# Building a product of two weight matrices: the second operand turned by VectorE instead of TensorE

## What is computed

```python
# part 1 (64 experts)
h   = silu(inp @ wg[e]) * (inp @ wu[e]);  out_e = h @ wd[e]
x   = x + scatter(out_e * weight)

# part 2: x is [32, 128, 1024]
H      = einsum('btd,od->bto', x, W)          # + rank-16 adapter picked per batch
result = einsum('bsd,od->bso', H, base_w) + base_b
logits = H @ router_w.T + router_b            # top 2 of 8
x      = x + result + 2 * gated (H @ lora_A) @ lora_B
```

## Time and profile before

| | us |
|---|---|
| median of 3 runs | 2355.13 |
| lowest, highest | 2351.75, 2357.51 |
| the profiled execution, device time | 2365.02 |
| its span in the trace | 2363.3 |
| TensorE busy | 2326.7 (98%) |
| VectorE busy | 1780.2 (75%) |
| ScalarE busy | 1418.5 (60%) |

### The profile page before, as it was taken

How to read it: one execution, slowest core, us unless ns; L and a number is a source line. 1 busy time by engine, 2 the same in 40 slices (tenths; PEclk the granted TensorE clock), 3 DMA queues, 4 the chain that set the end, 5 groups by cost and what they waited for, 6 DMA issues and landing times.

```text
span 2363.3 us, 35497 instructions
## 1 busy us (share of the span) xinstructions
PE 2326.7 (98%) x12594; PEld 2044.4 (87%) x12594; DVE 1780.2 (75%) x3091; ACT 1418.5 (60%) x2349; POOL 1343.8 (57%) x999
## 2 busy tenths in 40 slices
PE   6989999999999999999999999999999999999999
PEld 4768788888888888888888888888889999999999
DVE  4887788888888888888888888888863267666665
ACT  4766677777767777777777776777763122222221
POOL 4117888777777777877778777787730011111110
PEclk9999999999999999999999999999999999999999
DMA  8999899989999989989899899899886444544452
GB/s 300 380 311 335 257 281 288 287 272 292 279 289 290 281 276 283 286 280 279 276 291 282 275 285 279 281 282 287 274 255 140 103 110 131 144 131 132 132 140 83
DMA packets 250307, 582.35 MB, mean 246 GB/s; under 512 B 82697, under 2 KB 106634, under 8 KB 250130
## 3 DMA queue, kind: packets, MB, share of 16 engines
q1 hardware_dynamic: 183154, 401.18, 51.6%
q0 software_dynamic: 55584, 160.02, 26.2%
q10 hardware_dynamic: 11392, 18.88, 2.1%
HBM read 456.25 MB, written 123.45 MB: 245 GB/s over the span
## 4 chain that ended last, share of the span: by engine, by line
PE 94%; DVE 2%; issue 2%; ACT 1%; DMA 1%; ACTq 0%; POOL 0%; SPq 0%; DVEq 0%; POOLq 0%
PE ps L861 26%; PE ps L874 22%; PE ps L860 13%; PE ps L986 9%; PE ps L979 7%; PE ps L931 5%; PE ps L857 4%; PE ps L730 2%; PE ps L969 2%; PE ps L858 2%; PE ps L740 1%; PE ps L943 1%; PE ps L753 1%; PE ps L752 0%; ACT HR L1215 0%
## 5 line engine op out<-in xcount | busy, mean ns | idle before, releaser
L861 PE MATMUL ps<-XX,HR 128*128 128x512 f32 x2688 | 959.7, 396 | 0.0
L632 POOL DMA_INDIRECT Xg<-yd,idx x504 | 659.3, 1308 | 161.1 <-issue 152.7
L860 PE MATMUL ps<-XX,LR 128*128 128x256 f32 x2688 | 750.4, 279 | 0.1
L1747 DVE TENSOR_TENSOR LR<-raw,HR 128x1536 fp32r<-128x1536 f32 x384 | 657.8, 1751 | 10.1 <-ACT HR L1215 9.1
L861 PEld LDWEIGHTS ps<-XX,HR 128*128 128x128 f32 x2688 | 505.1, 188 | 104.2
L1215 ACT ACTIVATE HR<-raw 128x1536 fp32r<-128x1536 f32 x384 | 557.0, 1478 | 22.5 <-DMA raw<-in_L_ffn_wd 17.5
L860 PEld LDWEIGHTS ps<-XX,LR 128*128 128x128 f32 x2688 | 507.6, 189 | 18.3 <-DVE LR L1747 0.7
L654 POOL DMA_INDIRECT accd<-ot,toki x128 | 252.9, 1976 | 150.0 <-ACT ot L1269 127.8
L874 PE MATMUL ps<-LR,hH 128*128 128x512 f32 x768 | 303.3, 395 | 0.0
L874 PE MATMUL ps<-HR,hH 128*128 128x512 f32 x768 | 299.8, 390 | 3.0 <-DVE hL L1793 2.2
L874 PE MATMUL ps<-HR,hL 128*128 128x512 f32 x768 | 301.8, 393 | 0.0
(11 more groups left out here) (252 smaller groups left out, 3869.1 us busy)
## 6 DMA issues: line engine op xcount, KB each, us to landing
raw<-in_L_ffn_wd SPq DMA_DIRECT2D x128, 768.0 KB
raw<-in_L_ffn_wg SPq DMA_DIRECT2D x126, 768.0 KB
raw<-in_L_ffn_wu SPq DMA_DIRECT2D x126, 768.0 KB
yd<-yrow ACTq DMA_DIRECT2D x32, 512.0 KB
x<-accd SPq DMA_DIRECT2D x32, 512.0 KB, 3.9
out<-x SPq DMA_DIRECT2D x31, 512.0 KB, 5.2
xt<-in_x SPq DMA_DIRECT2D x25, 512.0 KB
accd<-xt SPq DMA_DIRECT2D x25, 512.0 KB
```

The lines of the kernel that those rows point to most:

```text
L632: eng.indirect_dma_start(Xg[:, c, q, :], None, yd4, bass.IndirectOffsetOnAxis(ap=idx4[:, e % 4, i:i + 1], axis=0))\
L860: eng.matmul(bank(out, 0, CAP), wl, xx[:, 0:CAP], start=False, stop=False)
L861: mm = eng.matmul(bank(out), wh, xx, start=False, stop=(k == 7))
L1747: eng.tensor_tensor(LR[:, (n + 2) % NHL, :], raw[:, n % NRAW, :], HR[:, (n + 2) % NHL, :].bitcast(F32), ALU.subtract).then_inc(s_L, 1)
```

## The change

`base_w` is loaded in partition groups: for each row block j four DMAs of 32 partitions (`load_b`), each in 1 KB pieces, so that 32 x 32 turns within VectorE's transpose give a contraction index in another but consistent order. W, router_w, lora_A and Bm are loaded in that same order, each DMA becoming four. The DMAs of `base_w` go to `Xg` and `XR` (blocks 0 to 3), free once the last expert's input is split, and to `x1` and `x45` (4 to 7). VectorE turns them (`turn_b`) at three places of the last expert, and the high and low parts are made from these turned blocks (`high_b`, `low_b`). TensorE keeps only the eight small transposes of the router. Block 0 of the weight stage runs by column groups, each with a wait of its own. Three orders change: ScalarE splits the last `dB` before the results of expert 62; the low parts of tile 4 come before `low_g(3)` and `low_T(2)`; `take(p, 1)` comes before the turns of tiles 6 and 7.

```diff
@@ SyncE
-            eng.wait_ge(s_dn, 4 * (E - 1))
-            for j in range(3):
-                load_b(j)
+            def load_b(j, there):
+                for f in range(4):
+                    eng.dma_start(base_in(j)[32 * f:32 * f + 32, :].rearrange("s (q c) -> s q c", q=4),
+                                  base_w[j * P:(j + 1) * P, f * 256:(f + 1) * 256].rearrange("(q s) c -> s q c", q=4))\
+                       .then_inc(there, 16)
+            eng.wait_ge(s_vl, 2 * E)
+            for j in range(4):
+                load_b(j, d_bw[0])
             eng.wait_ge(s_L, len(units) - 2)
-            eng.dma_start(x1[0:NA, 2, :], router_w).then_inc(d_bw[3], 16)
-            load_b(3)
-            load_b(4)
+            load_b(4, d_bw[1])
+            load_b(5, d_bw[1])
...
             eng.wait_ge(s_L, len(units))
-            for j in range(5, 8):
-                load_b(j)
+            load_b(6, d_bw[2])
+            load_b(7, d_bw[2])
@@ TensorE
-                        if e == E - 1:
-                            for n in ([o], [4 + 2 * o, 5 + 2 * o], [12 + o])[j]:
-                                turn_b(n)
+                        if e == E - 1 and j == 0 and o == 0:
+                            turn_router()
...
+                if j == 0:
+                    eng.wait_ge(s_gs, 3 * E)
+                    for g, (a, z) in enumerate(CG):
+                        eng.wait_ge(s_bl, (5, 8, 10)[g])
+                        for q in range(8):
...
@@ ScalarE
+                    if e == E - 1:
+                        split("dB", e)
                     for o in range(4):
                         result(e - 1, o // 2, o % 2)
...
+            high_router()
+            for j in range(7):
+                high_b(j)
...
@@ VectorE
+            def turn_b(j):
+                eng.wait_ge(d_bw[max(0, j // 2 - 1)], 64 * (4 if j < 4 else 2))
+                if j >= 5:
+                    eng.wait_ge(s_bt, j)
+                eng.transpose(base_t(j), base_in(j)).then_inc(s_bt, 1)
...
+                if e == E - 1:
+                    eng.wait_ge(s_dn, 4 * (E - 1))
+                    turn_b(0)
+                    turn_b(1)
+                    turn_b(2)
+                    split("dB", e)
                 join(3 * e)
...
+                    turn_b(3)
+                    turn_b(4)
+                    turn_b(5)
                 join(3 * e + 1)
...
+                    turn_b(6)
+                    turn_b(7)
                     low_w(0)
                 join(3 * e + 2)
...
+            low_r(4, 0)
+            low_r(4, 1)
+            low_g(3)
             low_T(2)
-            low_g(3)
             low_T(3)
...
+                take(p, 1)
                 if p == ND:
                     turn_r(t1 + 2)
                     turn_r(t2 + 2)
-                take(p, 1)
```

More of the change, by code:

```diff
@@ L372, in wait_retired, with base_in, base_t, base_4 @@
                 eng.wait_ge(s_up, 3 * (e + 1))
-        XB = [0, 1, 4, 5, 3]
-        def base(j):
+        def base_in(j):
+            if j < 2:
+                return Xg[:, j, :, :].rearrange("p q s -> p (q s)")
+            if j < 4:
+                return XR[:, j - 2, :, :, :].rearrange("p q j t -> p (q j t)")
+            return x1[:, j - 4, :] if j < 6 else x45[:, j - 6, :]
+        def base_t(j):
             if j < 3:
                 return xbA[:, j, :]
-            s = XB[j - 3]
-            return x1[:, s, :] if s < 4 else x45[:, s - 4, :]
-        def base_group(j):
-            return 0 if j < 3 else 1 if j < 5 else 2
+            if j == 3:
+                return bt3[:, :]
+            return (x1[:, 3, :], x1[:, 0, :], x1[:, 1, :], x45[:, 0, :])[j - 4]
+        def base_4(j):
+            return base_t(j).rearrange("p (q j t) -> p q j t", q=4, j=8)
+        def base_dst(Y, j):
+            return Y[:, :, j * P:(j + 1) * P].rearrange("p j (q t) -> p q j t", q=4)
         def bcast(ap1, n):
@@ L925, in _ @@
                 b0 = mbank(j)
-                for q in range(8):
-                    if j == 0 and q == 4:
-                        eng.wait_ge(s_bl, 18)
-                    for m, (X, Y) in enumerate([(WH, BH), (WH, BL), (WL, BH)]):
-                        for g, (a, z) in enumerate(CG):
-                            mm = eng.matmul(bank(b0 + g, 0, z - a), X[:, j % 2, q, :], Y[:, q, a:z],
-                                            start=(q == 0 and m == 0), stop=(q == 7 and m == 2))
+                if j == 0:
+                    eng.wait_ge(s_gs, 3 * E)
+                    for g, (a, z) in enumerate(CG):
+                        eng.wait_ge(s_bl, (5, 8, 10)[g])
+                        for q in range(8):
+                            for m, (X, Y) in enumerate([(WH, BH), (WH, BL), (WL, BH)]):
+                                mm = eng.matmul(bank(b0 + g, 0, z - a), X[:, 0, q, :], Y[:, q, a:z],
+                                                start=(q == 0 and m == 0), stop=(q == 7 and m == 2))
+                else:
+                    for q in range(8):
+                        for m, (X, Y) in enumerate([(WH, BH), (WH, BL), (WL, BH)]):
+                            for g, (a, z) in enumerate(CG):
+                                mm = eng.matmul(bank(b0 + g, 0, z - a), X[:, j % 2, q, :], Y[:, q, a:z],
+                                                start=(q == 0 and m == 0), stop=(q == 7 and m == 2))
                 mm.then_inc(s_m, 1)
@@ L1360, in _ @@
                         high_x(e + 1, 1)
-                    split("dB", e)
+                        split("dB", e)
                     copy_2(3 * e)
@@ L1897, in _, with low_b @@
                 split(k, 3)
+            def turn_b(j):
[3 more added lines that the diff above has]
+                eng.transpose(base_t(j), base_in(j)).then_inc(s_bt, 1)
+            def low_b(j):
+                eng.wait_ge(s_bh, j + 2 if j < 7 else 10)
+                eng.tensor_tensor(base_dst(BL, j), base_4(j), base_dst(BH, j).bitcast(F32), ALU.subtract)\
+                   .then_inc(s_bl, 1)
             def low_w(j):
@@ L1918, in _ @@
                 low_h(3 * e)
-                split("dB", e)
+                if e < E - 1:
+                    split("dB", e)
+                else:
+                    turn_b(3)
+                    turn_b(4)
+                    turn_b(5)
                 join(3 * e + 1)
```

128 lines of the change are left out of this document (56 added, 72 removed).

## The result

The changed kernel takes 2360.78 us (median of 11 executions, 2356.91 to 2364.76) against 2355.77 (median of 11, 2351.59 to 2358.82) for the kernel before on the same chip: a ratio of 1.0021, 95% interval 1.0013 to 1.0030. It is 5.0 us slower, which is inside the 0.3% that the prediction named as "no change". 7.0 us of work left TensorE, and more than 7 us of waiting and half-rate time came in.

The account below looks back on a forecast made before the run. TensorE's queue was taken to bound the kernel. Its 7.0 us saved are taken back by the wait for the loads: block 0 +5.4, reordered steps -1.5, sum +3.9 on 2355.13 gives 2359.0 us, range 2354.5 to 2365.5.

Parts of the forecast that it names:

- T0: Time when base_w blocks 0 to 3 have landed and VectorE's first turn can start: 1771.5, bounds 1769.5 to 1777.
- company: Term of T0: expert 62's scatter beside the loads slows their last 0.8 MB, giving 1771 to 1772.5 before landing.
- Alone: Term of T0: the four blocks at 210 GB/s without the scatter beside them, 1769.1 before 0.5 us for landing.
- The rule of the ports: Loads over 32 partitions reach 8 of SBUF's 16 DMA ports, 218 GB/s; at 392 the sum would be below -2 us.
- From T0 to block 0: VectorE's chain of turns, split, joins and low parts before block 0's first column group: 25.3 us, start at 1796.8.
- Both just arrive: Blocks 4 and 5 land at 1778, needed at 1780.5; blocks 6 and 7 at 1784, needed at 1785.3.
- it would be ready before VectorE and wait again: TensorE finishes the last expert at 1792.1 and waits for VectorE until block 0 at 1796.8.
- I cost it at nothing: Half clock after TensorE's wait costs 1.5 to 3 us, covered by 4.7 us to spare before block 0: zero.
- the half rate reaches block 0: Rival: TensorE's clock falls in the wait and stays low into block 0, adding 2 us, 2361; chance 0.05.
- what is late next: Last stage, p = 2: after both waits go, low_T(3) comes 1.2 us later, first used after the 48 direct matmuls.
- slow rate: Rival: loads run at mixed small pieces' 153 GB/s, T0 = 1777, +9.4 us, 2364.5, or 2367 with a second wait; chance 0.30.
- In time: Rival: loads land by 1759, block 0 starts at 1784.3, time 2346.6; needs T0 under 1761 to win 7 us; chance 0.07.

Follow-up runs that it names:

- e5: Changed kernel with the scatter of expert 62 held back until blocks 0 to 3 of base_w have landed; ratio 1.0023 against the kernel before.
- e2: Changed kernel with each base_w DMA writing 1 KB pieces to all 128 partitions, second part's output wrong; ratio 1.0021 against the kernel before.
- e6: Changed kernel with both 128-partition base_w loads and the scatter of expert 62 held behind blocks 0 to 3; ratio 1.0012 against the kernel before.
- e10: As e9, but blocks 0 and 1 share one semaphore and blocks 2 and 3 have one each; 2353.22 us, ratio 0.9994 against the kernel before.
- e9: Changed kernel with base_w reordered memory to memory beforehand, each block then one 128-partition DMA of 4 KB rows; 2353.51 us, ratio 0.9997 against the kernel before.
- e4: Changed kernel with 22, 4 and 8 small unread matmuls in TensorE's three waits; 2357.69 us, ratio 1.0018 against the kernel before.
- e8: Changed kernel with block 0 in the old order, waiting for all ten low parts; 2366.17 us, ratio 1.0050 against the kernel before.
- e7: Kernel before with only the reordered steps of the last stage; 2353.97 us, ratio 1.0001 against the kernel before.
- e12: As e11, plus 4 and 8 small unread matmuls in TensorE's waits; 2351.09 us, ratio 0.9985 against the kernel before.
- e11: As e10, with the first W block's high and low parts made at the last expert's start; 2351.61 us, ratio 0.9987 against the kernel before.
- e3: Changed kernel with the four partition groups of a block issued in order 0, 2, 1, 3; 2356.16 us in one execution.

## Why the prediction was right

The class, "no change", and the time (2359.0 forecast, 2360.78 measured) hold, and the mechanism is the one forecast: a wait for the loads in VectorE's queue takes back what TensorE saved. That the number comes so close is in part luck, since errors of up to 1.5 us went both ways (see the sum below). Point by point:

- **What TensorE loses.** The 16 groups of transposes are gone; this is 7.0 us less work, as the sum had it.
- **T0.** Forecast 1771.5; the turn starts at 1761.81, which is 1770.1 on the clock of before (8.32 us later). The rate was right: 221 and 224 GB/s against 210. The issue took 8.9 us instead of 7.4, but ended 5.5 us before the turn and set nothing. The term **company** was wrong: I charged 2 to 3.4 us for the scatter (and used the low end: with the landing it would have been 1771.5 to 1773), and e5 shows that holding the scatter back gains nothing. It was issued about when forecast, from 1755.3 on (1763.6 on the clock of before), but its two DMAs landed 9.6 us after their issue (median), later than the turn. Between 1750.8, where `dB` ends, and the turn the DMAs moved about 2.5 MB, of which the four blocks are 2.1. "Alone" plus landing, 1769.6, would have been the better value by the prediction's own working. The row of 273 GB/s against 392 on which I rested the term was of whole-block loads, and for loads over all partitions e2 and e6 show that the scatter does cost, about 3.5 us.
- **The rule of the ports.** The prediction weighed the Trainium skill's rule ("SBUF — State Buffer", section on the DMA port swizzle) against the 392 GB/s of the whole blocks. The runs settle it: 340 (e2) and 405 GB/s (e10) over all partitions, some 220 over 32. Its other side was that at 392 the change would come out at -2 us; e9, the same with whole-block loads, came out at 0.9997, which is -0.7 us, with an interval that includes -2.
- **From T0 to block 0.** Forecast 25.3 (the terms listed there add up to 25.2); measured 25.8 (1761.81 to 1787.64). Most of the difference is a wait that the prediction took as just avoided ("Both just arrive"): the turn of block 4 waits 0.69 us for its load. Blocks 6 and 7 were in time. Block 0 at 1787.64 is 1796.0 on the clock of before; forecast 1796.8. The two errors partly cancel.
- **TensorE's waits.** Block b = 2 was forecast at 1777.4 with a wait of 7.7; it started at 1775.9 on the clock of before with 6.1, earlier by the error in T0. The further wait that was forecast ("it would be ready before VectorE and wait again"), 4.7 us ahead of block 0, came in two parts, 1.2 us before the last step of `down` and 2.3 before block 0; the rest went into matmuls at half rate.
- **The clock.** It fell in the wait as forecast, and the half rate there cost nothing (in e4, without it, block 0 begins no earlier). What failed is "I cost it at nothing" as a whole: it fell a second time, at the start of block 0, where nothing covers it, and took 1.5 us in the profiled execution. That is what the rival "the half rate reaches block 0" said (chance 0.05), and its 2361 is nearer to the measured 2360.78 than the forecast's 2359.0. By e4's ratio it is about 0.7 us on the mean, with an interval that includes zero.
- **Block 0 by column groups.** "No wait" between the groups: right. That the groups are worth about 7 us (e8) was not priced at all, since they were only asked for a cost.
- **lora_A and Bm.** TensorE has no wait in the expert loop from 400 us on; the zero holds. ScalarE's waits for `wd` between 560 and 800 are 8.2 us now against 11.1.
- **The reordered steps.** Forecast -1.5, measured -0.7 (456.5 to 455.8, and the same in e7). Both waits went, as forecast, but "what is late next" was answered with a step that is not used until later, and the trace has two others in their place, 0.29 and 0.57.
- **The sum.** +5.4 - 1.5 = +3.9 was forecast. Measured in the traces: +4.6 for the start of block 0, +1.5 for the clock, -0.7 for the orders, +5.4; in the medians +5.0. Measured less forecast, that is -0.8 in T0 and the chain (-1.4 and +0.5), +0.8 in the orders and +0.7 to +1.5 in the clock.

The rival "slow rate" lost at its deciding point: T0 would have had to be at 1774.6 or later. "In time" lost by 9 us.

Open stays why the medians of e4 and e12 gain less than their profiles, how often the clock falls within block 0, and what makes it fall there in some profiles and not in others. That blocks 4 and 5 delayed e9's first turn is read from the rates and was not tested by a run.

## What to carry to other kernels

A transfer has a rate that belongs to its shape: 1 KB pieces over 32 partitions ran at 220 GB/s with the DMA engines fully busy, whole blocks over 128 partitions at 405. If a layout needs the slow shape, rearrange the data once in memory while the DMAs have time, and load it fast where someone waits (e9, -5.7 us against the change by the ratios). Work moved to an engine with idle time is free only as long as its first instruction doesn't wait: here one turn that waited for a DMA stood in front of everything that TensorE needed. The faster load (e9), finer semaphores (e10) and work put into the wait (e11) together turned +5 us into -3; most of it is e9, and e10's share lies within the noise. Changing one of two limits can show nothing (e2, e5); only the pair (e6) shows what they are worth.

## What was not expected of the hardware

- The accumulating scatter of 1.05 MB makes no difference to when 32-partition loads at 220 GB/s have landed (e5), but beside loads over all partitions the total is 191 GB/s (e2), where the same loads without it run at 249 (e6), and the first turn comes 3.5 us later. With hardly any load beside it, it runs at 218 GB/s with a DMA share of 1.08 (e10, 1756 to 1761): it keeps the DMA engines as busy for half the bytes.
- TensorE's granted clock fell to 0.50 at the start of block 0 after waits of 1.2 and 2.3 us (after), or 0.42 and 2.31 us (e11). In e9 and e10 it fell 0.9 and 1.5 us after the block's start, with TensorE busy all that time. The row is e10's, whose block 0 starts at 1777.94:

```profile
1779.00:1780.00 1.00, 1.00 (x6) 1.00 (x5) 1.00 (x2) 1.00 (x2) 0.00 (x0) 0.72 0.07 19
```

  With small matmuls in those waits it stayed at 1.00 (e12). But e6 has the same 2.3 us wait ahead of block 0, with waits of 3.6 and 0.2 before it, no small matmuls, and no fall in block 0: what parts the two cases isn't shown.
- The order of the partition groups alone seems to change the rate of the loads: 247 GB/s (e3, one execution) against 216 to 223 in four profiles in the old order.
